# The key weights' split behind three query units, and the output bias added by GpSimd during the first values

## The reference, cut to what matters

```python
q = hidden_states @ Wq + bq          # Wq, Wk, Wv: 512 x 4096 (32 heads of 128)
k = hidden_states @ Wk + bk
v = hidden_states @ Wv + bv
q = rms_norm(q, gq); k = rms_norm(k, gk)   # over all 4096 columns
...
return out @ Wo + bo                 # and x = x + that
```

## Time and profile before

| | |
|---|---|
| median of 3 runs | 2321.61 us (2321.32 to 2323.63) |
| profiled execution | 2324.25 us, its span 2322.5 us |
| busy in the span | PE 2256.0 (97%), DVE 1609.4 (69%), ACT 1135.6 (49%), POOL 828.8 (36%) |
| mean granted clock of TensorE | 0.989 of full |

### The profile page before, as it was taken

One profiled execution on the slowest core, in us unless ns is written; L12 is line 12 of the kernel. 1 busy time (PEld: TensorE's weight loads), 2 busy tenths in 40 slices (PEclk: granted clock), 3 DMA queues, 4 the chain that ended last, 5 costly groups with the idle time before them and its releaser, 6 DMA issues. The chain is left out here.

```text
span 2322.5 us, 34366 instructions
## 1 busy us (share of the span) xinstructions
PE 2256.0 (97%) x11044; PEld 1874.1 (81%) x11044; DVE 1609.4 (69%) x2654; ACT 1135.6 (49%) x1845; POOL 828.8 (36%) x736
## 2 busy tenths in 40 slices
PE   7899999999989999999999999999998999899998
PEld 5688888888778888888888888888886788687887
DVE  5544444444378888888888888888886665785765
ACT  3233332322266666666666666666663344352442
POOL 4553332233222222212212222222214466672565
PEclk9999999999999999999999999999999999999999
DMA  3155555455332211211221221221201111141210
GB/s 114 47 181 191 190 177 183 168 187 184 132 107 71 81 55 67 81 66 56 81 72 50 81 72 50 81 78 44 81 24 41 51 68 44 33 129 37 73 59 37
DMA packets 106182, 210.47 MB, mean 91 GB/s; under 512 B 9728, under 2 KB 42496, under 8 KB 102784
## 3 DMA queue, kind: packets, MB, share of 16 engines
q1 hardware_dynamic: 106112, 209.57, 26.9%
HBM read 140.33 MB, written 69.21 MB: 90 GB/s over the span
## 5 line engine op out<-in xcount | busy, mean ns | idle before, releaser
L1106 ACT ACTIVATE at_pT_hi<-ps 128x512 fp32r<-128x512 f32 x512 | 278.3, 595 | 352.3 <-PE ps L1210 352.2
L1148 DVE TENSOR_REDUCE at_small<-ps 128x1 f32<-128x1024 f32 x256 | 312.5, 1221 | 84.0 <-PE ps L402 83.0
L1158 DVE TENSOR_TENSOR at_pT_lo<-ps,at_pT_hi 128x512 fp32r<-128x512 f32 x512 | 327.1, 680 | 3.8 <-ACT at_pT_hi L1106 3.8
L1113 ACT ACTIVATE at_probs<-ps,at_small,cols 128x1024 f32<-128x1024 f32 x256 | 309.2, 1208 | 28.2 <-DVE at_small L1150 21.6
L865 POOL TENSOR_TENSOR qkv_acc<-qkv_acc,qkv_sq 128x512 f32<-128x512 f32 x128 | 166.2, 1299 | 320.1 <-ACT qkv_sq L755 316.5
L1210 PEld LDWEIGHTS ps<-ident,at_probs 128*128 128x128 f32 x2048 | 239.2, 140 | 37.9 <-issue 4.4
L1210 PE MATMUL ps<-ident,at_probs 128*128 128x128 f32 x2048 | 266.4, 273 | 3.2 <-DVE at_pT_lo L1158 3.2
L1172 DVE SCALAR_TENSOR_TENSOR x<-ps,at_small,x 128x512 f32<-128x512 f32 x256 | 192.0, 750 | 10.2 <-PE ps L402 3.1
L1043 POOL TENSOR_TENSOR at_o_lo<-at_o_raw,at_o_hi 128x512 fp32r<-128x512 f32 x32 | 41.2, 1288 | 439.8 <-ACT at_o_hi L1127 439.8
L402 PE MATMUL ps<-ln_xT_hi,ln_xT_lo 128*128 128x512 f32 x768 | 196.0, 390 | 0.0
L826 DVE TENSOR_SCALAR qkv_res<-ps,cols 128x512 f32<-128x512 f32 x128 | 94.9, 748 | 141.7 <-PE ps L402 122.7
(11 more groups left out here) (273 smaller groups left out, 5636.4 us busy)
## 6 DMA issues: line engine op xcount, KB each, us to landing
scratch_q_hi<-qkv_q_hi SPq DMA_DIRECT2D x64, 256.0 KB, 2.1
scratch_q_lo<-qkv_q_lo SPq DMA_DIRECT2D x64, 256.0 KB, 2.3
scratch_k<-qkv_res SPq DMA_DIRECT2D x64, 256.0 KB, 2.8
scratch_v<-qkv_res SPq DMA_DIRECT2D x64, 256.0 KB, 2.3
k_raw<-scratch_k SPq DMA_DIRECT2D x32, 512.0 KB, 3.8
at_v_raw<-scratch_v SPq DMA_DIRECT2D x32, 512.0 KB, 3.3
wq_raw<-in_Wq SPq DMA_DIRECT2D x8, 1024.0 KB, 6.5
qkv_w<-in_Wk SPq DMA_DIRECT2D x8, 1024.0 KB, 5.0
```

The source lines that it names most:

```text
L1106: nc.scalar.activation(pT2[jp][0][:, 4 * b:4 * b + 4, w * P:(w + 1) * P], T_BANKS[:, b * HALF:(b + 1) * HALF].rearrange("p (k n) -> p k n" ...
L1113: nc.scalar.activation(probs[l % 4][:], scores(l)[:], ACT.Exp, bias=nbias[:, l % 4:l % 4 + 1], scale=rq[:, l % NT:l % NT + 1], accum_out=s ...
L1148: nc.vector.reduce_max(maxes[:, l % 4:l % 4 + 1], scores(l)[:], AX.X).then_inc(s_max, 1)
L1158: nc.vector.tensor_tensor(pT2[jp][1][out], T_BANKS[:, b * HALF:(b + 1) * HALF].rearrange("p (k n) -> p k n", k=4), pT2[jp][0][out], ALU.su ...
```

## The change

In the first group and stage Q alone, the split of Wk is issued before unit 3 (`LATE = 3`) on ScalarE and on VectorE, no longer before unit 0. GpSimd's wait for bo and its eight adds to x stand behind the 16 sums of the first group. No instruction is added or taken away, the order on SP and TensorE is as it was, and so are all later groups.

```diff
--- before.py
+++ after.py
@@ -658,7 +658,7 @@
         k_in, q_in, bo_in, bv_in = sem("k_in"), sem("q_in"), sem("bo_in"), sem("bv_in")
         kn_done, k0_hi_done = sem("kn_done"), sem("k0_hi_done")
 
-        AT_SUMS, AT_SPREAD = 1, 3
+        AT_SUMS, AT_SPREAD, LATE = 1, 3, 3
         block = core.open_block(ctx)
         weights = [ins["Wq"], ins["Wk"], ins["Wv"]]
         bias, gain = [core.cols["bq"], core.cols["bk"]], core.cols["gq"]
@@ -736,11 +736,14 @@
             def body(g):
                 for t in (Q, K, V):
                     n = g * 3 + t
-                    if t < V:
+                    late = isinstance(g, int) and g == 0 and t == Q
+                    if t < V and not late:
                         split(n + 1, t + 1, g)
-                    elif not is_last(g):
+                    elif t == V and not is_last(g):
                         split(n + 1, Q, g + 1)
                     for u in range(UNITS):
+                        if late and u == LATE:
+                            split(n + 1, t + 1, g)
                         if t == V:
                             continue
                         m = g * 16 + t * UNITS + u
@@ -807,9 +810,12 @@
             def body(g):
                 for t in (Q, K, V):
                     n = g * 3 + t
-                    if t < V or not is_last(g):
+                    late = isinstance(g, int) and g == 0 and t == Q
+                    if not late and (t < V or not is_last(g)):
                         split(n + 1, (t + 1) % 3)
                     for u in range(UNITS):
+                        if late and u == LATE:
+                            split(n + 1, t + 1)
                         wait(v, proj_done, n * UNITS + u)
                         if 4 <= t * UNITS + u < UNITS + 4:
                             v.wait_ge(q_lo_done, g * UNITS + t * UNITS + u - 3)
@@ -850,11 +856,6 @@
                 nc.gpsimd.memset(acc[t][:], 0.0).then_inc(acc_done, 1)
             pool.wait_ge(acc_done, 2)
 
-            pool.wait_ge(bo_in, 16)
-            for t in range(NT):
-                nc.gpsimd.tensor_tensor(core.x[:, t, :], core.x[:, t, :], bo[:], ALU.add)
-
-
             def body(g):
                 for t in (Q, K):
                     for u in range(UNITS):
@@ -863,6 +864,10 @@
                         pool.wait_ge(acc_done, m + 2)
                         part = acc[t][:, (u % 2) * HALF:(u % 2 + 1) * HALF]
                         nc.gpsimd.tensor_tensor(part, part, sq[:, u % 2, :], ALU.add).then_inc(acc_done, 1)
+                if isinstance(g, int) and g == 0:
+                    pool.wait_ge(bo_in, 16)
+                    for t in range(NT):
+                        nc.gpsimd.tensor_tensor(core.x[:, t, :], core.x[:, t, :], bo[:], ALU.add)
 
             groups(pool, body)
             pool.wait_ge(k0_hi_done, 1)
```

## The result

The median after is 2313.64 us (7 runs, 2311.39 to 2315.43); before, beside it, 2323.18 (7 runs). The ratio is 0.9956, 95% interval 0.9945 to 0.9968, that is 7.4 to 12.8 us less. The forecast was 2311.6, 10.0 less than the 2321.6 of before, with a range of 2308.8 to 2315.2.

A forecast was written before the change was run, and what follows sets the result against it. TensorE, 97% busy, was taken to lose time waiting for a bias eviction behind the key-weight split: 7.1 us stall, 2.7 slow clock, 0.26 slip make 10.0 off 2321.61, giving 2311.6, range 2308.8 to 2315.2.

The forecast's parts named there:

- The stall goes: TensorE at query unit 4: eviction 0 comes right behind the gains, so the wait goes, gaining 7.1 us.
- The slow clock: Query units 4 and 5, run at a lowered clock after the stall: 2.7 us gained (2.56 and 0.12).
- The slip: Key unit 4's first matmul, late behind GpSimd's adds and the third square: 0.26 us gained.
- Square 2 wants GpSimd's first sum, which nothing precedes any more: ScalarE's third query square: first sum ends at 108.4, square 2 at 109.5, then the keys' high part.
- The adds' new place: GpSimd's eight adds behind the 16 sums, 13.4 us into 22.50 us of idle time: cost 0.
- the collision: Adds against VectorE's low part of the next query weights: 0.7 us taken, 3.2 us of cover at value unit 4.
- no streak of adds: Rule of the shared port: VectorE late by whole adds, a streak if GpSimd always wins; by single ones, 2312.0.
- The stores: First query stores meet the Wv and bv loads: 6.8 us, back at 114.5, wanted about 115.9; priced at nothing.
- The rival of eviction 3: Query unit 7 waits for a late eviction 3, up to 2 us: gain 8, 2313.6; chance 0.08.
- Its clause that a stall of 2 us leaves the clock alone: Within a stall of up to 2 us at query unit 7, the clock would not have fallen yet.
- The total: Whole kernel: 10.0 us less than the 2321.61 median, giving 2311.6; range 2308.8 to 2315.2.
- the narrow band of 2309.5 to 2313.5: Total time if the forecast itself holds, allowing for the runs' spread and clock recovery; chance 0.86.

The follow-up runs named there:

- e3: Kernel before plus 30 unused matmuls ahead of TensorE's wait at query unit 4; first to value matmul 49.89 us, ratio to before 1.0011.
- e5: Kernel before with the bias adds moved and 27 unused matmuls ahead of the wait at query unit 4; 44.75 us to first value matmul, ratio 0.9972.
- e2: Kernel before with only the eight bias adds moved behind the first group's sums; 47.10 us to first value matmul, ratio to before 0.9992.
- e1: Changed kernel with the bias adds put back ahead of the sums, so only the split moved; 52.87 us to first value matmul, ratio to before 1.0019.
- e7: Changed kernel with LATE = 6, the key split ahead of query unit 6; 41.65 us to first value matmul, ratio to before 0.9976.

## Why the prediction was right, and where it was not

- **The stall goes.** Predicted 7.1 us at once, eviction 0 right behind the gains; measured so (106.18, straight after 106.10). In time from the start of the block the steps were: high part of the keys 7.8 (measured 7.58), low part 9.8 (9.51), eviction 3 done 12.8 (12.80), first value matmul 38.2 (38.18). One duration was off: the low part took 2.62, not 2.29, and the three sums took 4.44 us and ended only at 112.78, inside it. That the 12.8 was met so closely is luck: the low part began 0.29 sooner than predicted and took 0.33 longer.
- **The slow clock.** Predicted 2.7. Between the two kernels it is that: the first key matmul stands 26.20 and 16.42 us into the block, 9.78 less, of which 7.10 are the stall (114.24 - 107.14), so 2.68. Filling the stall gives less, 2.46 in e3 and 2.35 in e5. Some of the difference is seen: unit 4 behind the filler still takes 2.86 in both, not 2.72, and in e2, to which e5 is compared, the slow clock cost only 2.42.
- **The slip.** 0.26 was right as a term of this sum. What the prediction did not say is that the two edits can't be added: alone they gain -4.65 (e1) and +1.12 us (e2), together +10.04. It priced the adds' move by what it freed in the trace of before, and there the stall hid what the adds would cost once it was gone. The step "Square 2 wants GpSimd's first sum, which nothing precedes any more" did hold this dependence, without the price of its absence.
- **The adds' new place.** Predicted to cost nothing, and it costs nothing, but the collision was priced too low. 0.7 us was taken; the low part of the next query weights took 3.27 instead of 2.47, and behind it a copy of 128x4 took 1.26 us, where such copies take 0.16 in the later groups. The cover went from 3.2 us to 2.4 (eviction 148.81 + 0.69 = 149.5 against value unit 4 at 140.98 + 10.88 = 151.86). The copy, with one input, I had not thought of. The Trainium skill, SBUF — State Buffer, section "Who interferes with whom", names copies among the operations that can take the port which VectorE shares with GpSimd. The trace agrees: this copy takes 1.26 us in all seven traces with the adds in the values, and at most 0.17 in before and e1, and 1.26 is less than one add here, 12.08 / 8 = 1.51. Each of the two instructions was late by less than one add (the low part by 0.98 against its mean of 2.29, the copy by 1.10), but both were, and they add up; no streak of adds held either.
- **The stores.** The bound of 6.8 us behind a 1 MB load was the right one: the first query unit's two stores took 6.6 and 6.8 us after, and 6.7 and 6.9 in e7. ScalarE does wait for a store, 1.03 us at the last query unit after, and e7 shows that it matters as soon as nothing else fills the time.
- **The rival of eviction 3** was rightly small: it was done at 115.60, and unit 7 began at 119.22 - 2.72 = 116.50, 0.9 later as predicted. Its clause that a stall of 2 us leaves the clock alone was not tested; the shortest wait here behind which the clock fell is 2.52 us (below).
- **The total.** 9.5 us between the medians and 10.04 in the run-up agree within the interval. The median itself, 2313.64, is 2.0 above the forecast of 2311.6: 1.6 of it because the kernel before came out higher over seven runs than over the first three (2323.18, 2321.61), the rest the 9.5 for 10.0. It lies in the range, but 0.1 outside the narrow band of 2309.5 to 2313.5, and on the 2313.6 of the rival of eviction 3. By the time alone the two could not be told apart; the trace decides, as unit 7 did not wait.

## What to carry to other kernels

Work that nobody needs yet must not stand ahead of the first instruction that lets TensorE go on, and where it may stand is read from two sides: what it waits for, and what the ring of buffers behind it bears; between the two its place is worth nothing. A short slip just after a long stall is worth a look, for it can be the edge of a second limit, and then two edits have to be made together: here one alone made the kernel slower and the other did next to nothing. An independent stage of idle time is the right cover for deferred work, and its true length is found by making that work longer.

## What was unexpected in the hardware

The length of a wait does not tell in these traces whether the clock falls. In e3 a wait of 2.52 us was followed by a stretch at 0.50, which began only after the matmuls had begun again. In e7 one of 3.17 us, up to 121.81, was not, as the windows over and behind it show:

```profile
118.00:122.00 4.00, 0.83 (x4) 0.38 (x3) 2.54 (x2) 1.43 (x1) 1.17 (x1) 1.00 0.38 146
122.00:126.00 4.00, 4.00 (x18) 3.30 (x18) 2.40 (x4) 3.48 (x5) 2.08 (x2) 1.00 0.46 171
```

Nor does one kind of stall meet the fall at one time. In the kernel before TensorE is idle from 107.30 on and the clock falls in 109:110; in e2 it is idle from 107.97 on, and the clock is at 1.00 until 112:

```profile
112.00:113.00 1.00, 0.00 (x0) 0.00 (x0) 1.00 (x1) 0.00 (x0) 0.00 (x0) 0.69 0.91 367
```

The clock also fell without a wait: in the windows from 613 to 622 us above TensorE is busy for all of the time, with the 128x1 matmuls of `sums` when it falls. What decides whether and when it falls stays open here.

And eight adds of 128x512 on GpSimd took 9.90 us beside an idle VectorE (e1), 12.08 in the values (after), and 13.37 beside the split and the evictions (before).
